# A causal attention whose four batches run interleaved, with the mask of its exp tiles added in PSUM by TensorE

## The reference

```python
h = _layernorm(x, ln_w, ln_b)                     # once more, after a first layer norm
h = causal depthwise convolution of h, 3 taps
q, k, v = jnp.split(h @ attn_w, 3, axis=-1)       # 16 heads of 8
q = q * cos + _rotate_half(q) * sin               # the same for k
scores = jnp.einsum('bqhd,bkhd->bhqk', q, k) / jnp.sqrt(8)
scores = jnp.where(causal, scores, -1e30)         # 512 x 512 for each batch and head
p = jax.nn.softmax(scores, axis=-1)
x1 = x + jnp.einsum('bhqk,bkhd->bqhd', p, v) @ proj_w
```

## Time and profile before

| | |
|---|---|
| median of three runs | 2458.39 us (2457.35 to 2462.53) |
| the profiled execution, first to last instruction (its span) | 2453.4 us; the page gives no other time for it |
| busy in the span | PE 86%, DVE 63%, ACT 53%, POOL 2% |
| chain that ended last | PE 68%, DVE 16%, ACT 10%, issue 4% |
| the attention of the first stage C | from 1061.5 to 1414.6 us |
| the attention of the second stage C | from 1886.8 to 2240.1 us |

### The profile page before, as it was taken

How to read it: one execution, slowest core, us unless ns; L and a number is a source line. 1 busy time by engine, 2 the same in 40 slices (tenths; PEclk the granted TensorE clock), 3 DMA queues, 4 the chain that set the end, 5 groups by cost and what they waited for, 6 DMA issues and landing times.

```text
span 2453.4 us, 25839 instructions
## 1 busy us (share of the span) xinstructions
PE 2111.8 (86%) x8484; PEld 1128.1 (46%) x8484; DVE 1551.6 (63%) x2648; ACT 1289.2 (53%) x2038; POOL 58.0 (2%) x44
## 2 busy tenths in 40 slices
PE   6999999999999799967977978867996878978887
PEld 5886444444444478723333356631222333233665
DVE  5887445654445678784675556658887674664665
ACT  5997556655555689835435444453113436435443
POOL 0000000000000000040000000000004000000000
PEclk8999999999999899968668779985557667768999
DMA  3441000000000143200000011000000000000110
GB/s 83 72 75 37 15 1 15 15 15 15 15 0 9 21 76 72 56 1 1 0 0 0 0 35 45 15 7 3 2 28 0 1 0 0 0 0 11 55 30 17
DMA packets 59405, 51.73 MB, mean 21 GB/s; under 512 B 1184, under 2 KB 54816, under 8 KB 59360
## 3 DMA queue, kind: packets, MB, share of 16 engines
q1 hardware_dynamic: 59360, 51.18, 9.5%
HBM read 49.53 MB, written 1.64 MB: 21 GB/s over the span
## 4 chain that ended last, share of the span: by engine, by line
PE 68%; DVE 16%; ACT 10%; issue 4%; DMA 2%; DVEq 0%; ACTq 0%; SPq 0%
PE ps L385 9%; PE ps L387 8%; PE ps L386 8%; PE ps L825 7%; PE ps L1057 5%; PE ps L639 4%; PE ps L232 4%; PE ps L632 3%; DVE arena L974 3%; PE ps L815 3%; PE ps L798 2%; PE ps L801 2%; ACT rstd L249 2%; PE ps L776 2%; ACT rstd L245 2%
## 5 line engine op out<-in xcount | busy, mean ns | idle before, releaser
L483 DVE TENSOR_TENSOR hid_lo<-arena,hid_hi 128x512 fp32r<-128x512 f32 x384 | 259.1, 688 | 74.3 <-ACT arena L440 72.3
L385 PE MATMUL ps<-x_hi,w_hi 128*128 128x512 f32 x512 | 213.7, 417 | 53.5 <-DVE arena L557 51.1
L890 ACT ACTIVATE arena<-ps 128x1024 f32<-128x1024 f32 (+3 forms) x256 | 177.6, 705 | 77.6 <-PE ps L815 72.7
L988 DVE SCALAR_TENSOR_TENSOR arena<-arena,con 128x256 f32<-128x256 f32 x256 | 109.0, 426 | 167.1 <-ACT arena L890 163.9
L387 PE MATMUL ps<-x_hi,w_lo 128*128 128x512 f32 x512 | 208.7, 408 | 0.0
L386 PE MATMUL ps<-x_lo,w_hi 128*128 128x512 f32 x512 | 208.4, 407 | 0.0
L437 ACT ACTIVATE hid_hi<-ps,wslot 128x512 fp32r<-128x512 f32 x256 | 182.5, 713 | 46.6 <-PE ps L387 28.9
L974 DVE TENSOR_REDUCE arena<-ps 128x2 f32<-128x1024 f32 (+3 forms) x256 | 195.3, 818 | 15.6 <-PE ps L801 7.7
L825 PE MATMUL ps<-arena 128*32 128x256 f32 (+3 forms) x1024 | 197.0, 471 | 1.4
L440 ACT ACTIVATE arena<-ps,wslot 128x512 f32<-128x512 f32 x256 | 181.5, 709 | 4.3 <-DVE hid_lo L483 4.3
L385 PE MATMUL ps<-hid_hi,w_hi 128*128 128x512 f32 x384 | 155.2, 404 | 14.6 <-DVE hid_lo L483 14.6
(11 more groups left out here) (208 smaller groups left out, 3700.6 us busy)
## 6 DMA issues: line engine op xcount, KB each, us to landing
gate_bc<-gates_dram SPq DMA_DIRECT2D x24, 1024.0 KB, 14.9
wslot<-pack_a SPq DMA_DIRECT2D x16, 514.5 KB, 3.4
wslot<-pack_b SPq DMA_DIRECT2D x8, 901.5 KB, 4.6
wslot<-pack_c SPq DMA_DIRECT2D x8, 768.0 KB, 4.3
res<-x_in SPq DMA_DIRECT2D x4, 256.0 KB, 4.9
out_dram<-res SPq DMA_DIRECT2D x4, 256.0 KB, 2.8
con<-consts_dram SPq DMA_DIRECT2D x1, 439.0 KB, 3.9
bc_dram<-arena SPq DMA_DIRECT2D x1, 384.0 KB, 3.4
```

The lines of the kernel that those rows point to most:

```text
L385: pe.matmul(ps[:, bank, :], w1, hi, start=start, stop=False)
L483: dve.tensor_tensor(hid_lo[item % 2][:, k, :], hid32[:, k, :], hid_hi[item % 2][:, k, :].bitcast(F32), ALU.subtract).then_inc(S["hid_ok"], 1)
L890: act.activation(pt[:, u % NPT, :, 0:n], ps[:, 2 * (u % 2):2 * (u % 2) + 2, 0:n], ACT.Exp, scale=SCALE).then_inc(S["exp_ok"], 1)
```

## The change

- **Batches are interleaved.** The work of phases 1 and 2 ("side" work) of batch b + 1 is cut into 60 uses of two PSUM banks (5 and 6) and dealt out over 16 steps; phase 3 of batch b ("main" work) has one step for each group of four heads and key tile. At each step PE does the scores of the next step, some side uses, and the values of this one. The side work of batch 0 stands alone ahead of it, and the main work of batch 3 has no side work. The loops over batches are written out, and keys, values and second queries have two buffers.
- **The maxima** have one bank for each use, four, two or one head in it: 44 uses for a batch, with 512 columns for DVE to reduce, or 384 for the third tile.
- **The mask of the exp tiles** is two more matmuls for each pair of heads (`mask_qk16` as the weights, the identity moving), accumulated in PSUM on the scores ahead of exp. L988 and its table `tri` are gone. (No GpSimd select stood in the kernel before.)
- **The values** are four heads at once, in four column groups of one bank (bank 4). Phase 4 is done for four heads at a time (`turned`, bank 7), spread over later steps.
- **The start.** DVE makes the convolution of batch 0 in three instructions (`dve_conv`), and GpSimd that of the others. GpSimd writes the padding (`pool_pads`), as soon as x is there. PE reads the convolution directly, without the copy L869.
- Buffers move: `gate_bc` and `bc_row` now lie in a larger `arena`. The other stages keep their instructions.

The diff, cut to its core:

```diff
+STEPS = 4 * TPB
+USES = 60
+TURNS = 6
...
+SIDE_USES = ([("qkv", 0, 0), ("qkv", 1, 0), ("key", 0, 0), ("query", 0, 0), ("qkv", 2, 0)]
+             + [("max", 0, u) for u in range(4)]
+             + [("key", 1, 0), ("query", 1, 0), ("qkv", 3, 0), ("again", 0, 0)]
+             + [("max", 1, u) for u in range(8)]
+             + [("key", 2, 0), ("query", 2, 0), ("again", 1, 0)]
+             + [("max", 2, u) for u in range(8)]
+             + [("key", 3, 0), ("query", 3, 0)]
+             + [("max", 2, u) for u in range(8, 16)]
+             + [("max", 3, u) for u in range(2)] + [("again", 2, 0)]
+             + [("max", 3, u) for u in range(2, 16)] + [("again", 3, 0)])
+USE_AT = {use: n for n, use in enumerate(SIDE_USES)}
+USES_BY_STEP = [2, 4, 9, 13, 18, 23, 26, 29, 37, 43, 47, 49, 55, 59, 60, 60]
...
-    pe.wait_ge(S["pad_ok"], 2 * c["attn"] + 2)
-    with pe.Fori(0, NB) as b:
-        q = 4 * c["attn"] + b
-        pe.wait_ge(S["hc_ok"], q + 1)
...
+    def side(b, n):
+        q = q0 + b
+        kind, i, u = SIDE_USES[n]
+        bank = side_bank(n)
+        if USES * q // 2 + n // 2:
+            pe.wait_ge(S[f"side_free{n % 2}"], USES * q // 2 + n // 2)
+        if kind == "qkv":
+            if i == 0:
+                pe.wait_ge(S["conv_all"], q + 1)
+            mm = pe.matmul(ps[:, bank, 0:3 * P], hc_all[:, b, i * P:(i + 1) * P], pcol("wqkv"),
+                           start=True, stop=True)
+        elif kind in ("key", "query", "again"):
+            if kind == "again":
+                pe.wait_ge(S["m_ok"], 4 * q + i + 1)
+            else:
+                pe.wait_ge(S["split_ok"], 4 * q + i + 1)
+            first = HEADS if kind == "key" else 0
             to = ps[:, bank, :].bitcast(BF16)
             for hp in range(PAIRS):
-                at = qk16[:, i, kind * HEADS + 2 * hp:kind * HEADS + 2 * hp + 2, :].rearrange("p h d -> p (h d)")
+                at = qk16[:, i, first + 2 * hp:first + 2 * hp + 2, :].rearrange("p h d -> p (h d)")
                 mm = pe.transpose(to[:, hp * P:(hp + 1) * P], at, ident16[:, :])
...
+        else:
+            if u == 0:
+                done = USE_AT["query", i, 0]
+                pe.wait_ge(S[f"side_free{done % 2}"], USES * q // 2 + done // 2 + 1)
+                done = USE_AT["key", i, 0]
+                pe.wait_ge(S[f"side_free{done % 2}"], USES * q // 2 + done // 2 + 1)
+            heads = max_heads(i, u)
+            keys = (i + 1) * P
+            for m, h in enumerate(heads):
+                r0 = 64 * (h % 2)
+                pe.matmul(ps[:, bank, m * keys:(m + 1) * keys], qt_s[r0:r0 + QROWS, h // 2, i * P:(i + 1) * P],
+                          kt_s[b % 2][r0:r0 + QROWS, h // 2, 0:keys], start=(m == 0), stop=False,
+                          skip_group_check=True)
+            edge = ps[:, bank, 0:len(heads) * keys].rearrange("p (m k) -> p m k", k=keys)[:, :, i * P:(i + 1) * P]
+            mm = pe.matmul(edge, ident16[:, :], mask_qk16[:, :].unsqueeze(1).to_broadcast([P, len(heads), P]),
+                           start=False, stop=True, skip_group_check=True)
+        mm.then_inc(S["side_mm"], 1)
...
+    def scores(b, j):
+        q, g, k = q0 + b, j // TPB, j % TPB
+        n = SEQ - k * P
+        for r in range(2):
+            hp = 2 * g + r
+            if 32 * b + 2 * j + r >= 2:
+                pe.wait_ge(S["exp_ok"], 32 * q + 2 * (j - 1) + r + 1)
             for jj in range(2):
                 r0 = 64 * jj
-                pe.matmul(ps[:, 2 * (u % 3) + jj, 0:(i + 1) * P], qt_s[r0:r0 + QROWS, hp, i * P:(i + 1) * P],
-                          kt_s[r0:r0 + QROWS, hp, 0:(i + 1) * P], start=True, stop=False)
+                pe.matmul(ps[:, 2 * r + jj, 0:n], kt_s[b % 2][r0:r0 + MROWS, hp, k * P:(k + 1) * P],
+                          q2_s[b % 2][r0:r0 + MROWS, hp, k * P:SEQ], start=True, stop=False)
             for jj in range(2):
-                mm = pe.matmul(ps[:, 2 * (u % 3) + jj, i * P:(i + 1) * P], ident16[:, :], mask_qk16[:, :],
-                               start=False, stop=True)
...
+                mm = pe.matmul(ps[:, 2 * r + jj, 0:P], mask_qk16[:, :], ident16[:, :], start=False, stop=True)
             mm.then_inc(S["s2_mm"], 1)
...
-        def scores(u):
-            k, hp = UNITS[u]
-            n = SEQ - k * P
-            if u == 0:
-                pe.wait_ge(S["q2_ok"], 4 * q + 4)
-            for jj in range(2):
-                r0 = 64 * jj
-                mm = pe.matmul(ps[:, 2 * (u % 2) + jj, 0:n], kt_s[r0:r0 + MROWS, hp, k * P:(k + 1) * P],
-                               q2_s[r0:r0 + MROWS, hp, k * P:SEQ], start=True, stop=True)
...
-        def values(u):
-            k, hp = UNITS[u]
-            pe.wait_ge(S["sel_ok"], 32 * q + u + 1)
-            for jj in range(2):
-                g, at = (2 * hp + jj) // 4, 32 * ((2 * hp + jj) % 4)
-                mm = pe.matmul(ps[at:at + 32, 4 + g, k * P:SEQ], vc[:, k, 2 * hp + jj, :],
-                               pt[:, u % NPT, jj, 0:SEQ - k * P], start=(k == 0), stop=(k == TPB - 1),
-                               skip_group_check=True)
-            mm.then_inc(S["pv_mm"], 1)
...
+    def values(b, j):
+        q, g, k = q0 + b, j // TPB, j % TPB
+        if k == 0 and 4 * b + g:
+            pe.wait_ge(S["pvs_ok"], 4 * q + g)
+        pe.wait_ge(S["exp_ok"], 32 * q + 2 * j + 2)
+        for m in range(4):
+            mm = pe.matmul(ps[32 * m:32 * m + 32, 4, k * P:SEQ], vc[b % 2][:, k, 4 * g + m, :],
+                           pt[:, (2 * j + m // 2) % NPT, m % 2, 0:SEQ - k * P], start=(k == 0),
+                           stop=(k == TPB - 1), skip_group_check=True)
+        mm.then_inc(S["pv_mm"], 1)
...
+    pe.wait_ge(S["pad_ok"], c["attn"] + 1)
+    pe.wait_ge(S["ln_log"], 4 * c["ln"] + 8)
+    for n in range(USES):
+        side(0, n)
+    scores(0, 0)
+    for b in range(NB):
+        for j in range(STEPS):
+            if j + 1 < STEPS:
+                scores(b, j + 1)
+            if b + 1 < NB:
+                for n in range(USES_BY_STEP[j - 1] if j else 0, USES_BY_STEP[j]):
+                    side(b + 1, n)
+                if j + 1 == STEPS:
+                    scores(b + 1, 0)
+            values(b, j)
+            if j in (5, 9, 13):
+                turned(b, j // 4 - 1)
+            if b and j in (1, 3, 4):
+                turned(b - 1, {1: 3, 3: 4, 4: 5}[j])
+    for m in range(3, TURNS):
+        turned(NB - 1, m)
...
+    def exps(b, j):
+        q, n = q0 + b, SEQ - j % TPB * P
+        for r in range(2):
+            u = 2 * j + r
+            act.wait_ge(S["s2_mm"], 32 * q + u + 1)
+            if 16 * q + j >= 2:
+                act.wait_ge(S["pv_mm"], 16 * q + j - 1)
+            act.activation(pt[:, u % NPT, :, 0:n], ps[:, 2 * r:2 * r + 2, 0:n], ACT.Exp,
+                           scale=SCALE).then_inc(S["exp_ok"], 1)
...
+    for j in range(STEPS):
+        side(0, j)
+    for b in range(NB):
+        for j in range(STEPS):
+            exps(b, j)
+            if j % TPB == 0 and 4 * b + j // TPB:
+                if j:
+                    summed(b, j // TPB - 1)
+                else:
+                    summed(b - 1, 3)
+            if b and j == 4:
+                y_turned(b - 1)
+            if b + 1 < NB:
+                side(b + 1, j)
+    summed(NB - 1, 3)
+    y_turned(NB - 1)
...
+def pool_pads(pool, c):
+    for v in vc:
+        pool.memset(v[:, :, :, DH:DH + 1], 1.0)
+        pool.memset(v[:, :, :, DH + 1:32], 0.0)
+    pool.memset(qk16[:, :, HEADS:2 * HEADS, QROWS:MROWS], 1.0)
+    pool.memset(qk16[:, :, 0:HEADS, QROWS:64], 0.0)
+    pool.memset(qk16[:, :, HEADS:2 * HEADS, MROWS:64], 0.0).then_inc(S["pad_ok"], 1)
...
+def dve_conv(dve, c):
+    w = pcol("conv_c")
+    h, to = ha[:, 0, :], hc_all[:, 0, :]
+    done = 2 * c["attn"]
+    dve.wait_ge(S["ln_out"], 4 * c["ln"] + 5)
+    dve.tensor_scalar(to, h, w[:, 2:3], None, ALU.mult).then_inc(S["tap_now"], 1)
+    dve.wait_ge(S["tap_now"], done + 1)
+    dve.scalar_tensor_tensor(out=to[:, 1:SEQ], in0=h[:, 0:SEQ - 1], scalar=w[:, 1:2], in1=to[:, 1:SEQ],
+                             op0=ALU.mult, op1=ALU.add).then_inc(S["tap_now"], 1)
+    dve.wait_ge(S["tap_now"], done + 2)
+    dve.scalar_tensor_tensor(out=to[:, 2:SEQ], in0=h[:, 0:SEQ - 2], scalar=w[:, 0:1], in1=to[:, 2:SEQ],
+                             op0=ALU.mult, op1=ALU.add).then_inc(S["conv_all"], 1)
...
+    def maxima(b, i, units):
+        keys = (i + 1) * P
+        for u in units:
+            bank, free = filled(b, "max", i, u)
+            heads = max_heads(i, u)
+            step = heads[1] - heads[0] if len(heads) > 1 else 1
+            dve.tensor_reduce(neg_max[:, i, heads[0]:heads[-1] + 1:step],
+                              ps[:, bank, 0:len(heads) * keys].rearrange("p (m k) -> p m k", k=keys), AX_X, ALU.max,
+                              negate=True).then_inc(free, 1)
...
+    for j in range(STEPS):
+        side(0, j)
+    for b in range(NB):
+        for j in range(STEPS):
```

(31 more changed lines are left out.)

405 lines of the change are left out of this document (220 added, 185 removed).

## The result

The kernel after takes 2492.64 us (median of 4, 2490.45 to 2495.09) against 2458.61 us (4 runs): 1.0139 times as long, 95% interval 1.0125 to 1.0154. It is 34 us slower, where 98 us faster had been forecast. Its span is 2492.0 us.

What follows compares the result with a forecast made beforehand. No engine fills a batch, so phases behind one another were the cost. Per attention 58 + 3 x 72 + 34 = 308 us against 353, starting 4 earlier: 49 saved, 98 in both, giving 2360 us (range 2270 to 2440).

Steps and rivals of the forecast that it cites:

- Start, gain 4 us: First projection: PE begins 4 us earlier, as memsets leave DVE and the convolution needs no GpSimd or copy.
- PE's prices and four column groups: Main work: prices at 2.4 GHz; four heads' values side by side, 0.99 us for 512 columns.
- B: Values: four column groups run two by two, 11 us more a batch, 2440 us in all; chance 0.09.
- PE's work of 62 us at 2.4 GHz, stalls of 9 to 10: Interleaved batch: 62 us of main and side work on PE plus 9 to 10 of stalls, 72 us.
- The clock: the step that failed: Interleaved batches: PE's clock low in the first quarter, 1.00 behind it, since a bounding PE is never idle.
- Rival C: Interleaved batches: clock stays at 1.2 GHz, 100 us a batch, 43 lost per attention, 2540 us; chance 0.08.
- Masks and maxima: Interleaved batch: new exp masks take 7 us of PE; the 44 maxima uses take 25 us.
- the turn of two banks: Maxima: fill, mask, wait and reduction take 1.4 us for two uses, so 0.70 a use.
- First side work 58, last main work 34: Ends of each attention: first side work alone 58 us, last main work alone 34 in place of 38.
- The rule of the Trainium skill on changes of the tiling mode: PE: changing tiling mode drains it, about 0.1 us each, some 200 times a batch, already inside the prices.

Runs made afterwards that it cites:

- e3: Kernel after with an unused 512-column product ahead of each of the 44 uses of the maxima: 2495.9 us.
- e16: Kernel after with an unused 128-column product ahead of each use of the maxima: 2528.7 us.
- e8: Kernel before, not interleaved, with its exp mask moved from VectorE to TensorE and no select: 2507.6 us.
- e1: Kernel after without the 32 pairs of mask products ahead of exp in each batch: 2438.7 us.
- e7: Kernel after without the masks in the maxima, exp masks kept: 2447.5 us.
- e10: Kernel after with maxima uses issued in pairs in interleaved batches only, and no masks in the maxima anywhere: 2397.9 us, ratio 0.9752.
- e4: Kernel after with the next batch's side work behind all of a batch's main work instead of between its steps: 2525.4 us.
- e5: Kernel after with maxima uses issued two at a time, even and odd heads alternating on two row groups into both side banks, spread over the step: 2455.5 us.

## Why the prediction was wrong

*Start, gain 4 us.* Right: from the end of VectorE's layer norm to the first projection it is 2.5 us (1057.35 to 1059.82) for 6.6 before. The stages ahead end 2.4 us later, so PE began only 1.7 us earlier.

*PE's prices and four column groups.* Right to 0.02 us, and B is out.

*PE's work of 62 us at 2.4 GHz, stalls of 9 to 10.* That PE is idle 9 to 10 us is in part luck. The forecast was for 2.4 GHz, with some 5 us of waits for banks inside the 62, so some 15 of idle time; at the low clock PE's longer work covers part of it, and in the fastest records below PE is idle 12. The work can be bounded: the fastest of the six records of each step (three batches in both attentions) sum to 7.11 + 4.73 + 5.28 + 6.57 + 3.20 + 10.09 + 3.37 + 1.80 + 6.53 + 3.27 + 9.02 + 1.85 + 2.38 + 6.78 + 6.56 + 1.17 = 79.7 us, with some steps still partly at 1.2 GHz (steps 5, 10 and 13 at 0.67, 0.81 and 0.79). Steps 9, 11 and 12 take 11.42 us cold and 7.50 hot, 1.5 times; by that the three would lose another 4 to 5, an estimate of 75. e3's batch without its fillers is 78 or more at 0.90. A batch at full clock is 75 to 80, not 72.

*The clock: the step that failed.* "Its clock low in their first quarter and 1.00 behind it", from "once PE is the bound it is never idle, and the values, in every step, are what raised the clock". Measured by steps in the first interleaved batch it is nearly the other way round: 0.55 and 0.77 in steps 0 and 1, 0.87 to 1.00 in steps 2 to 4 and 6 to 8, but 0.50 to 0.52 in 9 to 14, where PE is hardly ever idle. Of the 19 us between 91 (the six batches' mean) and 72, at least 11 are the clock's (91 to 79.7), and 15 to 16 by the estimate; the rest, 3 to 8, are terms a little too small. Rows 9 showed a rise beside values of 512 columns; I took from it that a busy PE is granted the full clock. e16 against e3 refutes that: 90% busy either way, 0.70 and 0.90.

The Trainium skill (TensorE: Matmul & The Clock Gate, What's actually happening) has the clock follow from how busy PE has been. By its rule steps 9 to 14, 98% busy, would have run at 2.4 GHz; the trace has 0.51 there, and the measurement decides.

Rival C had this mechanism, and its edge: "from about 87 us a batch on, which is a clock at the low level in a little over half of it". At 0.70 it is 60% of the time, and 91 us; its own price, the low level throughout (100 us a batch, 2540), was too high. I gave it 0.08 with the argument above against it, although showed 0.54 with PE 87% busy in just these instructions.

*Masks and maxima.* The masks' 7 us a batch (e8: 6.3; e1: 7.5 in the mean) were in the sum, rightly. The maxima were priced by the turn of two banks, 0.70 a use; at the low clock PE's 0.76 to 0.79 is over it, and PE, not the banks, sets the pace (pairs give 7.5 us a batch back at the same clock, e7 against e10). The loss of the pair was not in the sum as a cost.

*First side work 58, last main work 34.* 64 and 39 in the first attention, 62 and 38 in the second. The first attention is 64 + 275 + 39 = 378 us and the second 370, against 308 forecast for each: 132 us, the whole miss.

*The rule of the Trainium skill on changes of the tiling mode* was inside the measured prices and says nothing on the miss.

*What the change does.* It is not the overlap that costs time but its price: with one head at a time and masks on PE, the engine that is the bound is busy 81 us of a batch for 73 before, at a clock that falls there. Of the 42 us that the two attentions lost, 25 are in the two first side works, where nothing overlaps (64 and 62 us for the 50.4 of the earlier trace rows), and 15 in the six interleaved batches (91 for 88). e4 to after is what overlap gives (33 us), e1 what the masks of exp cost (54), e7 what those of the maxima cost (45), e7 to e10 what one head at a time costs in the batches (50).

## What to carry to other kernels

Where a change makes TensorE the bound, price its work at both clock levels, and take the level from the stretch of before whose instructions the new stretch will consist of (here 0.54 in the maxima before, 0.50 in steps 9 to 14), not from its busy share. Move masks to TensorE only where it is not the bound (they cost their full 0.22 us a pair in e8). When two heads on two row groups become one head at a time, count the lost pair; and when two banks are filled at once, check that another engine does not then take turns with PE (e5's first stretch, 78 for 64 us).
